# A macaron layer on one core: two `xhat` buffers, transposes two steps of the tile later, GpSimd's blocks spread over the steps, variance terms on VectorE

## What is computed

```python
x = x + 0.5 * ffn(layernorm(x))        # ffn normalises once more, and adds its own input
x = x + mixer(layernorm(x))
x = x + 0.5 * ffn(layernorm(x))

def ffn(x):                            # H = 256, F = 1024, integer weights with scales per group of 128
    h = layernorm(x) * gamma + beta
    y = silu(h @ dequant(fc1_q, fc1_scales) + fc1_bias)
    z = y @ dequant(fc2_q, fc2_scales) + fc2_bias
    return x + 0.5 * z

def mixer(x):                          # N = 64
    a, b, c = sigmoid(x @ Wa + ba), x @ Wb + bb, tanh(x @ Wc + bc)
    s[t] = a[t] * s[t-1] + (1 - a[t]) * b[t]
    return (c * s) @ Wy + by + x @ Wd + bd
```

## Time and profile before

| | us |
|---|---|
| median of 3 runs | 741.83 (740.2 to 741.88) |
| the profiled execution, its own time | 739.66 |
| its span in the trace | 737.8 |
| first feed-forward stage | about 17 to 308 |
| mixer | about 308 to 442 |
| second feed-forward stage | about 442 to 738 |

### The profile page before, as it was taken

How to read it: one execution, slowest core, us unless ns; L and a number is a source line. 1 busy time by engine, 2 the same in 40 slices (tenths; PEclk the granted TensorE clock), 3 DMA queues, 4 the chain that set the end, 5 groups by cost and what they waited for, 6 DMA issues and landing times. The chain is left out here.

```text
span 737.8 us, 13716 instructions
## 1 busy us (share of the span) xinstructions
PE 698.3 (95%) x3250; PEld 539.9 (73%) x3250; DVE 627.5 (85%) x1216; ACT 637.0 (86%) x1052; POOL 623.6 (85%) x800
## 2 busy tenths in 40 slices
PE   4899999999999999989999997999999999999996
PEld 3577777777777777767788874777777777777774
DVE  6599998999999988688777785999999998999886
ACT  4889899998998999688888878889999899998984
POOL 5899999999999988767666658999999999999963
PEclk9999999999999999999999999999999999999999
DMA  8640000000000000000000000001110000000001
GB/s 259 205 140 1 1 0 0 0 0 0 0 0 0 1 1 0 1 1 1 0 0 0 1 0 1 2 28 35 44 37 28 28 29 28 28 30 28 30 30 59
DMA packets 19674, 19.96 MB, mean 27 GB/s; under 512 B 1532, under 2 KB 19378, under 8 KB 19634
## 3 DMA queue, kind: packets, MB, share of 16 engines
q1 hardware_dynamic: 19536, 19.48, 8.3%
q10 hardware_dynamic: 98, 0.02, 0.0%
HBM read 11.11 MB, written 8.39 MB: 26 GB/s over the span
## 5 line engine op out<-in xcount | busy, mean ns | idle before, releaser
L690 DVE SCALAR_TENSOR_TENSOR z_acc<-ps_z,cols,z_acc 128x512 f32<-128x512 f32 x448 | 322.5, 747 | 55.2 <-PE ps_z L902 24.5
L393 POOL TENSOR_TENSOR g_lo<-g_full,g_hi 128x512 fp32r<-128x512 f32 x256 | 329.5, 1293 | 36.2 <-ACT g_hi L562 35.4
L902 PE MATMUL ps_z<-g_hi,q_sb 128*128 128x512 f32 x512 | 210.8, 412 | 16.1 <-ACT z_acc L552 8.4
L560 ACT ACTIVATE g_full<-ps_fc,safe_scale 128x512 f32<-128x512 f32 x256 | 178.6, 698 | 51.9 <-PE ps_fc L902 38.6
L902 PE MATMUL ps_fc<-h_hi,q_sb 128*128 128x512 f32 x512 | 215.1, 420 | 4.8 <-ACT ps_fc L545 4.1
L902 PE MATMUL ps_fc<-h_lo,q_sb 128*128 128x512 f32 x512 | 203.6, 398 | 0.0
L902 PE MATMUL ps_z<-g_lo,q_sb 128*128 128x512 f32 x512 | 202.1, 395 | 0.0
L562 ACT ACTIVATE g_hi<-ps_fc,safe_scale 128x512 fp32r<-128x512 f32 x256 | 178.5, 697 | 0.0
L902 PEld LDWEIGHTS ps_z<-g_hi,q_sb 128*128 128x128 f32 x512 | 96.0, 187 | 69.5 <-ACT z_acc L552 22.4
L545 ACT ACTIVATE ps_fc<-ps_fc,bias,ratio 128x512 f32<-128x512 f32 x160 | 122.2, 764 | 1.4 <-DVE bias L785 1.4
L902 PEld LDWEIGHTS ps_fc<-h_hi,q_sb 128*128 128x128 f32 x512 | 97.2, 190 | 25.8 <-ACT ps_fc L545 4.1
(11 more groups left out here) (105 smaller groups left out, 813.8 us busy)
## 6 DMA issues: line engine op xcount, KB each, us to landing
resid<-in_L_attn_x SPq DMA_DIRECT2D x15, 512.0 KB, 4.2
out_x<-resid SPq DMA_DIRECT2D x15, 512.0 KB, 2.9
q_int<-in_L_ffn_fc_q SPq DMA_DIRECT2D x4, 512.0 KB, 7.0
resid<-in_L_attn_x SPq DMA_DIRECT2D x2, 256.0 KB, 3.0
out_x<-resid SPq DMA_DIRECT2D x2, 256.0 KB, 2.8
wd_sb<-in_L_attn_Wd SPq DMA_DIRECT2D x1, 256.0 KB
wy_raw<-in_L_attn_Wy SPq DMA_DIRECT2D x2, 64.0 KB
wab_sb<-in_L_attn_Wa SPq DMA_DIRECT2D x1, 64.0 KB
```

Of the source, the lines that this page charges most:

```text
L393: nc.gpsimd.tensor_tensor(g_lo[:, g % 4, :], g_full[:, g % 2, :], g_hi[:, g % 4, :].bitcast(F32), ALU.subtract).then_inc(g_ready, 1)
L560: nc.scalar.activation(g_full[:, g % 2, :], bank, ACT.Silu, scale=scale)
L690: nc.vector.scalar_tensor_tensor(out=z, in0=bank_of(g, n, par), scalar=col(R_S2 + KC * g + n), in1=z, op0=ALU.mult, op1=ALU.add).then_inc( ...
L902: last = nc.tensor.matmul(out, w, v, start=start and i == 0, stop=stop and i == len(pairs) - 1, skip_group_check=not start)
```

## The change

It changes the tables and with them what stands in which step, adds buffers and moves three small operations to another engine:

- `xhat` has two buffers (by the parity of the tile), so `normalise` waits for the `turn`s of two layer norms ago; `g_full` has four slots, so `silu(g)` waits for `g_low(g - 4)`.
- `turn` after steps 2 and 6 instead of 1 and 3 (c = 1 now waits for both `add_ffn` of the tile before), `turn_back` after 4 and 5 instead of 5 and 6, `round_h` and `lower_h` moved with them.
- GpSimd has one block of other work per step: `residual` one block in each of 0 to 3, `rsqrt` in 4, `normalise` one block in each of 5 to 7.
- The variance terms and the negated mean are made by VectorE, at the end of `variance`, in two slots by parity; `rsqrt` on GpSimd waits for them (`terms_ready`) and starts with the power. `variance` waits for its own `aggr_done`, and no longer for the terms of the `rsqrt` before.
- `scale_half` is on ScalarE for six steps (0, 1, 2, 3, 5, 7) instead of five, on VectorE for two (4, 6) instead of three.
- In step 4 ScalarE does the first of the two `first_sum` ahead of `silu(3)` and the second right behind it; before, both stood behind it, the second at the head of step 5.
- `statistics` in two halves in steps 1 and 2, `variance` in 4. In a stage's first tile `statistics` stands in step 5 and `variance` in 7 (before: 4 and 5), and `residual` in 2 and 3 (before: 4).

```diff
-    SCALED_ON_ACT = (0, 2, 4, 5, 6)
-    SCALED_ON_DVE = (1, 3, 7)
+    SCALED_ON_ACT = (0, 1, 2, 3, 5, 7)
+    SCALED_ON_DVE = (4, 6)
...
-    RESIDUAL_AT = (4, 1, 1)
-    RSQRT_AT = (5, 2, 2)
-    NORMALISE_AT = ((6, 7), (5, 6), (5, 6))
-    TURN_AT = ((3, 5), (1, 3), (1, 3))
+    RESIDUAL_AT = ({2: (0, 1), 3: (2, 3)},) + ({0: (0,), 1: (1,), 2: (2,), 3: (3,)},) * 2
+    RSQRT_AT = (5, 4, 4)
+    NORMALISE_AT = ({6: (0, 1), 7: (2,)},) + ({5: (0,), 6: (1,), 7: (2,)},) * 2
+    TURN_AT = ((3, 5), (2, 6), (2, 6))
...
-        xhat = sb("xhat", [P, SUB, D])
+        xhat = sb("xhat", [P, 2, SUB, D])
...
-        g_full = sb("g_full", [P, 2, TILE])
+        g_full = sb("g_full", [P, 4, TILE])
...
             def normalise(ln, t, par, blocks, signal):
...
-                wait(act, turned, 2 * ln)
+                wait(act, turned, 2 * ln - 2)
...
-                wait(act, g_ready, FC * ff + (g - 1))
-                nc.scalar.activation(g_full[:, g % 2, :], bank, ACT.Silu, scale=scale)
+                wait(act, g_ready, FC * ff + (g - 3))
+                nc.scalar.activation(g_full[:, g % 4, :], bank, ACT.Silu, scale=scale)
...
+            def variance(ln, par, twice=True):
 
                 dve.wait_ge(stats_done, ln + 1)
-                wait(dve, terms_ready, ln)
                 nc.vector.memset(wait_holder[:, :], 0.0)
                 for a in range(SUB):
                     last = nc.vector.bn_aggr(mean_var[:, a, :], stats[:, a, :])
                 last.then_inc(aggr_done, 1)
+                dve.wait_ge(aggr_done, ln + 1)
+                wait(dve, shift_ready, ln - 1)
+                if twice:
+                    nc.vector.tensor_scalar(var_terms[:, par, 0, :], mean_var[:, :, 1], 1.0 + EPS, EPS * EPS,
+                                            ALU.mult, ALU.add)
+                    nc.vector.tensor_scalar(var_terms[:, par, 1, :], mean_var[:, :, 1], 4.0, 4.0 * EPS,
+                                            ALU.mult, ALU.add)
+                else:
+                    nc.vector.tensor_scalar(var_terms[:, par, 0, :], mean_var[:, :, 1], 1.0, EPS, ALU.mult, ALU.add)
+                nc.vector.tensor_scalar(neg_mean[:, par, :], mean_var[:, :, 0], -1.0, 0.0, ALU.mult,
+                                        ALU.add).then_inc(terms_ready, 1)
...
-                            if f == TURN_AT[before][0]:
-                                wait(pe, ffn_added, 2 * ff - 2)
+                            c = TURN_AT[before].index(f)
+                            if c and before:
+                                pe.wait_ge(ffn_added, 2 * ff)
```

More of the change, by code:

```diff
@@ L340, in _, with rsqrt @@
             nc.gpsimd.memset(bias_raw[:, :, :], 0.0).then_inc(raw_zero, 1)
-            def rsqrt(ln, twice, shares=0):
-                pool.wait_ge(aggr_done, ln + 1)
+            def rsqrt(ln, par, twice, shares=0):
+                pool.wait_ge(terms_ready, ln + 1)
                 wait(pool, xhat_ready, ln)
@@ L449, in tile @@
                         else:
-                            rsqrt(ln0 + 1, True)
+                            rsqrt(ln0 + 1, 1, True)
                         if not before and f == 1:
-                            normalise(ln0 + 1, 1, halves[0])
+                            normalise(ln0 + 1, 1, 1, halves[0], True)
                         if ff0 == 0 and not behind and f in XN_LOWER_AT:
                             xn_low(0, 0, XN_LOWER_AT.index(f))
-                        if behind >= 1 and f == RESIDUAL_AT[before]:
-                            residual(ln + 1, t + 1, share(ln + 1, ff0))
+                        if behind >= 1 and f in residual_at:
+                            residual(ln + 1, t + 1, share(ln + 1, ff0), residual_at[f])
                         if behind >= 2 or ff0 == 0:
@@ L478, in mixer_tile @@
                 if behind:
-                    rsqrt(t + (NT + 2), behind == 1, 0 if before else NT + 2)
+                    rsqrt(t + (NT + 2), par, behind == 1, 0 if before else NT + 2)
                 for c in range(KC) if behind else ():
@@ L632, in mixer_tile @@
                 if behind:
-                    normalise(t + (NT + 2), 0 if behind == 1 else t + 2, range(SUB), xhat_ready)
+                    normalise(t + (NT + 2), 0 if behind == 1 else t + 2, par, range(SUB), xhat_ready)
                 else:
@@ L719, in tile @@
                                 add_mixer(NT - 1, 1, half)
-                        if ff0 == 0 and not behind and f == STATISTICS_AT:
+                        if ff0 == 0 and not behind and f == VARIANCE_AT:
                             lower_bias()
@@ L726, in tile @@
                             statistics(2)
-                            variance(ln0 + 2)
-                        if (behind >= 3 or ff0 == 0) and f == STATISTICS_AT:
-                            if behind >= 3 and ff0 == 0:
+                            variance(ln0 + 2, 0)
+                        statistics_at = STATISTICS_AT if before else {5: range(SUB)}
+                        if (behind >= 3 or ff0 == 0) and f in statistics_at:
+                            if behind >= 3 and ff0 == 0 and statistics_at[f][0] == 0:
                                 dve.wait_ge(x_loaded[1 - par], 8 * t + (32 if par == 0 else 40))
@@ L733, in tile @@
                                 dve.wait_ge(aggr_done, ln0 + 3)
-                            statistics(t + 3 if behind >= 3 else 2 - behind)
-                        if (behind >= 3 or ff0 == 0) and f == VARIANCE_AT:
-                            variance(ln + 3)
+                            statistics(t + 3 if behind >= 3 else 2 - behind, statistics_at[f])
+                        if (behind >= 3 or ff0 == 0) and f == (VARIANCE_AT if before else FC - 1):
+                            variance(ln + 3, 1 - par, behind >= 3)
                 if ff0 == 0:
@@ L887, in _, with turn @@
             nc.tensor.transpose(ps_tr2[:, 0:ROWS], rows[:, :], ident[0:ROWS, 0:ROWS]).then_inc(rows_turned, 1)
[L889 removed]
+            def turn(ln, par, c, bank=ps_tr, banks=1, shares=0):
                 pe.wait_ge(xhat_ready, ln + 1)
@@ L894, in turn @@
                 for a in range(SUB):
-                    last = nc.tensor.transpose(bank[:, a * P:(a + 1) * P], xhat[:, a, c * P:(c + 1) * P],
+                    last = nc.tensor.transpose(bank[:, a * P:(a + 1) * P], xhat[:, par, a, c * P:(c + 1) * P],
                                                ident[:, :])
@@ L1056, in mixer_tile @@
                     pe.wait_ge(ffn_added, 2 * NT)
-                turn(t + (NT + 1), 0, ps_tr, before)
-                turn(t + (NT + 1), 1, ps_tr2, 2)
+                turn(t + (NT + 1), 1 - par, 0, ps_tr, before)
+                turn(t + (NT + 1), 1 - par, 1, ps_tr2, 2)
                 if before == 2:
```

105 lines of the change are left out of this document (47 added, 58 removed).

## The result

The changed kernel takes 705.64 us (median of 4 runs, 705.11 to 706.08) against 741.02 for the kernel before (4 runs): a ratio of 0.9526, 95% interval 0.9503 to 0.9549. The forecast was 713 with a range from 706, so the direction was right and the gain 7 us too small. The profiled execution took 705.5 us, its span 703.7.

The account below looks back on a forecast made before the run. GpSimd and TensorE together were taken to set the 17.65 us tile. Savings of 21.6 (normal tiles), 2 (last tiles) and 4.8 (first tiles), 28.4 us, gave 711.3 from 739.66, plus 2.2 for the median: 713, range 706 to 736.

Parts of the forecast that it names:

- Floor of TensorE: Feed-forward tile: eight steps of 1.87 us and four transpose groups of 0.44 need 16.7 us of TensorE.
- Normal tiles: Both feed-forward stages: a tile falls from 17.65 to 16.75 us, over 24 tiles 21.6 us saved.
- 0.05 for missed rooms: Normal tile: 0.05 us added to the 16.7 floor for VectorE's smallest time margins, 0.2 and 0.3 us.
- GpSimd 16.0 us: Normal tile: GpSimd's work falls from 16.8 to 16.0 us without three small operations, 0.7 below the floor.
- 0.6 us of idle time: Normal tile: ScalarE, busy 16.1 of 16.7 us, keeps 0.6 us idle per tile to catch up.
- Rival C: Normal tile gets no shorter because ScalarE is next bound at 17.6 us; only first tiles gain, 736 us; chance 0.06.
- B: Rival: one new VectorE operation waits for a `g_low`, or ScalarE slips; tile 17.1 to 17.5, 722 to 733 us; chance 0.22.
- within 0.4 us: Sign that the forecast is right: VectorE's new operations at the end of `variance` take no more than this.
- Nothing on the path: Normal tile: two `xhat` buffers and moved transposes add no delay, since TensorE finds `xhat` ready a tile early.
- First tiles and stage ends: Feed-forward stages: first tiles save 2.4 us a stage, 4.8 in both; last two tiles 0.5 each, 2 us.
- Rival A: VectorE's new operations and GpSimd block each other; tile 18.2 us, kernel slower at 750 us; chance 0.11.
- Mixer: VectorE's two or three added small operations are covered by its 1.83 us idle; no change taken, 5 us if uncovered.

Follow-up runs that it names:

- a_slowpool: The changed kernel with one added GpSimd `memset` of 128x2048 into a spare buffer behind each `rsqrt`: 745.1 us (one run).
- a_resid4: The changed kernel with the four pieces of `residual` together in step 1 instead of one in each of steps 0 to 3: 714.0 us.
- a_best: The changed kernel with `g_full` in two slots and `variance` behind VectorE's fifth step instead of the fourth: 709.2 us.

## Why the prediction was right or wrong, point by point

- **Floor of TensorE: wrong, and the step that failed.** "Eight matmuls take 1.87 us" was read off the kernel before and taken as a property of the matmul. It is one of the matmul and of the addresses of its operands: the mean distance of 0.2329 us became 0.2290. 8 x 1.87 + 4 x 0.44 = 16.72 is met by `a_unalign` (16.66), the changed kernel with the addresses of before, whose 711.8 us stand 1.2 from the forecast 713. The address effect is 711.8 - 705.6 = 6.2 us, nearly the whole error of 7.4. The diff showed two small buffers growing; no term of the sum asked where things lie. That 711.8 comes so close to 713 is in part luck: against that kernel the normal tiles are forecast 2.2 us too small, and the first tiles and stage ends some 3 us too large. Why the addresses set the distance stays open.
- **Normal tiles.** Forecast 21.6 us, measured 28.8: (16.66 - 16.45) x 24 = 5.0 by addresses, (16.75 - 16.66) x 24 = 2.2 because the 0.05 for missed rooms was not needed and the floor of 16.7 came out 0.04 lower.
- **GpSimd 16.0 us: right** (`a_slowpool`: 17.83 - 1.81). That single blocks matter is right too (`a_resid4`, +8.3), but for another reason than `g_low`'s time: with one heavy piece it is VectorE's first new operation that waits longer for GpSimd.
- **ScalarE: right in that it doesn't bound.** It is fuller than forecast: 178.97 us busy of 180 are 16.4 us a tile, not 16.1, and the tile became shorter by 0.3 as well, so the 0.6 us of idle time did not come. Rival C is refuted, and B too as to the normal tile, which was not longer than forecast.
- **VectorE: right for the tile,** though the operations were mis-sized: 0.38 + 0.16 + 0.17 with overlaps, 0.54 us from first start to last end (forecast 0.35, bounds 0.35 to 0.8; the sign "within 0.4 us" did not come). That its rooms are small is borne out: three tiny operations more cost some 0.2 us a tile beyond the longer distance of the matmuls.
- **Moved transposes: mis-sized by their place in the text.** "Nothing on the path" is true after; the sum had their worth inside "the floor is reached". Undone they cost 14 us.
- **First tiles and stage ends: 6.8 us forecast, 5.3 measured.** The 3.47 us wait of VectorE and the 1.61 of TensorE went as said; two new waits of TensorE, 3.2 us in all, came in the second tiles, where VectorE stands behind GpSimd.
- **Rival A:** its mechanism is shown for one SBUF input, too. Its arithmetic is not: in a normal tile only the first operation waits. The Trainium skill's page "SBUF — State Buffer", section "Who interferes with whom", says the second to come is blocked until the first is done; the 0.38 and 0.71 us agree, and the 1.79 shows more than it says, that a waiting instruction can be passed by a second one of GpSimd. The 0.17 us inside the power of 1.64 us (`a_best`) does not agree.
- **Mixer: right.** From its first to its last `a_sb` on ScalarE it takes 435.50 - 312.25 = 123.25 us before and 420.15 - 297.13 = 123.02 after, with 603 matmuls in both:

```profile
312.25 0.69 ACT L617 ACTIVATE a_sb<-ps_z,cols 64x512 f32<-64x512 f32 x1 [2.28 <-PE ps_z L902]
435.50 0.68 ACT L617 ACTIVATE a_sb<-ps_z,cols 64x512 f32<-64x512 f32 x1 [1.16 <-PE ps_z L902]
```

```profile
297.13 0.68 ACT L606 ACTIVATE a_sb<-ps_z,cols 64x512 f32<-64x512 f32 x1 [2.29 <-PE ps_z L904]
420.15 0.68 ACT L606 ACTIVATE a_sb<-ps_z,cols 64x512 f32<-64x512 f32 x1 [1.20 <-PE ps_z L904]
```
